# Mamba mixers: the skip term moved from VectorE to TensorE and ScalarE, lent scans in place

## What is computed

```
xc, z = split(h @ inproj);  xc = silu(causal_conv(xc) + convb)
dt = softplus(x_proj part @ dtw + dtb);  Bm, Cm = other parts of x_proj
per time step:  dA = exp(dt * A);  h = dA * h + (dt * xc) * Bm;  y = sum over n of h * Cm
y = y + xc * D
y = y * silu(z);  out = y @ outproj
```

## Time and profile before

| | |
|---|---|
| median of 3 runs | 2694.64 us |
| profiled execution | 2695.85 us, span 2694.0 us |
| first Mamba stage, scans | from 66 us to 991 us of the span |
| second Mamba stage, scans | from 1974 us to 2434 us |
| a chunk, first scan to first scan of the next | 115.0 us (odd chunks, scans begin at a state) to 119.7 us (even) |
| busy shares of the span | TensorE 88%, VectorE 69%, ScalarE 50%, GpSimd 57% |

### The profile page before, as it was taken

How to read it: one execution, slowest core, us unless ns; L and a number is a source line. 1 busy time by engine, 2 the same in 40 slices (tenths; PEclk the granted TensorE clock), 3 DMA queues, 4 the chain that set the end, 5 groups by cost and what they waited for, 6 DMA issues and landing times. The chain is left out here.

```text
span 2694.0 us, 28358 instructions
## 1 busy us (share of the span) xinstructions
PE 2361.3 (88%) x8874; PEld 1077.4 (40%) x8874; DVE 1870.9 (69%) x2587; ACT 1339.3 (50%) x2213; POOL 1543.2 (57%) x1356
## 2 busy tenths in 40 slices
PE   7989899898988778888999769999889989688878
PEld 3323333333333223343433349998433333223322
DVE  2999999999999983347777241111379999994334
ACT  4556565655656443444666423332266556453333
POOL 2999999999999971150000112222179999992010
PEclk9999999999999999999999979999789999999989
DMA  4030412303031100043121059996332130300000
GB/s 179 25 125 1 143 52 84 133 10 125 1 125 52 74 0 24 19 123 63 38 39 25 6 188 329 327 329 233 105 126 79 48 125 1 125 1 22 1 9 32
DMA packets 70204, 239.03 MB, mean 89 GB/s; under 512 B 15819, under 2 KB 35799, under 8 KB 47399
## 3 DMA queue, kind: packets, MB, share of 16 engines
q1 hardware_dynamic: 58292, 183.90, 20.3%
q10 hardware_dynamic: 8018, 43.09, 4.6%
q0 software_dynamic: 3744, 10.23, 1.0%
HBM read 220.60 MB, written 16.38 MB: 88 GB/s over the span
## 5 line engine op out<-in xcount | busy, mean ns | idle before, releaser
L896 POOL TENSOR_TENSOR s_dbu<-s_dx,s_bc 128x512 f32<-128x512 f32 x768 | 968.6, 1290 | 26.4 <-DVE s_psum L564 24.8
L480 PE MATMUL s_psum<-s_hc,ident 128*128 128x512 f32 x1536 | 831.1, 634 | 151.9 <-DVE s_hc L584 131.2
L759 ACT ACTIVATE s_psum<-s_dt,s_a_neg 128x512 f32<-128x512 f32 x768 | 521.7, 688 | 576.9 <-DVE s_hc L584 576.0
L480 PEld LDWEIGHTS s_psum<-s_hc,ident 128*128 128x128 f32 x1536 | 263.8, 193 | 657.7 <-DVE s_hc L584 413.8
L584 DVE TENSOR_TENSOR s_hc<-s_psum,s_bc 128x512 f32<-128x512 f32 x624 | 419.8, 673 | 0.4 <-issue 0.4
L564 DVE TENSOR_TENSOR_SCAN s_psum<-s_psum,s_state,s_dbu 128x512 f32<-128x512 f32 x312 | 394.6, 1277 | 11.4 <-POOL s_dbu L896 6.7
L564 DVE TENSOR_TENSOR_SCAN s_psum<-s_psum,s_dbu 128x512 f32<-128x512 f32 x312 | 381.4, 1223 | 14.9 <-POOL s_dbu L896 12.5
L2015 ACT ACTIVATE s_probs<-s_banks 128x512 f32<-128x512 f32 (+3 forms) x384 | 169.6, 495 | 117.1 <-PE s_banks L1724 85.8
L2452 ACT ACTIVATE s_hidden<-s_banks,s_w 128x128 f32<-128x128 f32 x312 | 97.6, 364 | 194.3 <-PE s_banks L2244 192.5
L163 POOL TENSOR_TENSOR s_pair<-s_res 128x512 f32<-128x512 f32 x4 | 5.1, 1280 | 328.5 <-issue 327.1
L907 POOL TENSOR_TENSOR s_hc<-s_hs,s_bc 128x512 f32<-128x512 f32 x144 | 183.6, 1275 | 14.6 <-DVE s_hs L564 14.6
(11 more groups left out here) (325 smaller groups left out, 3272.6 us busy)
## 6 DMA issues: line engine op xcount, KB each, us to landing
s_bc<-fwd_rows SPq DMA_DIRECT2D x64, 1024.0 KB, 4.7
s_w<-in_moe_w SPq DMA_DIRECT2D x39, 1028.0 KB, 5.9
s_w<-in_moe_w ACTq DMA_DIRECT2D x39, 1024.0 KB, 6.8
s_bc<-m_rows SPq DMA_DIRECT2D x32, 1024.0 KB, 4.7
qk_parts<-s_parts SPq DMA_DIRECT2D x48, 128.0 KB, 1.9
s_stack_q<-qk_parts SPq DMA_DIRECT2D x96, 64.0 KB, 2.4
s_stack_k<-qk_parts SPq DMA_DIRECT2D x48, 128.0 KB, 4.4
x<-in_xT SPq DMA_DIRECT2D x4, 512.0 KB, 6.7
```

Of the source, the lines that this page charges most:

```text
L480: pe.matmul(psum[:, SCANS + block_no % 2, :], consts["ident"][:], hc[:, unit % PRODUCTS, :], start=(n == 0), stop=(n == NS - 1)).then_inc( ...
L759: act.activation(psum[:, unit % SCANS, :], dt[:, g % 2, i // NS, :], ACT.Exp, scale=a_neg[CHUNKS[g][0]][:, i:i + 1]).then_inc(decay_ready, 1)
L896: pool.tensor_tensor(dbu[:, unit % TERMS, :], dx[:, g % 2, i // NS, :], bc[:, 2 * n, :], ALU.mult)\
```

## The change

TensorE adds the skip: after the 16th product of a block it multiplies u with a 128x128 diagonal matrix of D, from a new tile `skip_in` with the four diagonals of a run, into the same PSUM sum. ScalarE's new `store_sum` copies the sum to dx, at i = 7, 23, 39 and 55 and once at the end; VectorE's `skip` is gone. `skip_in` is loaded by SP at the stage's start and, in the first stage, again for the second run. The lent scans write over their term in `dbu` and `hs` is gone; VectorE no longer waits before them. The term that takes a lent unit's slot, the next instruction of GpSimd after its lent product, waits for that product. The fourth gate product moves from i = 9 to i = 11.

```diff
+            sp.dma_start(skip_in[:], dram[f"{first}_skip"]).then_inc(skip_loaded, 16)
             sp.dma_start(w_out[:], dram[f"{first}_out"]).then_inc(out_loaded, 16)
...
             for g in range(NC):
+                if g and g % PER_RUN == 0:
+                    sp.wait_ge(skip_used, EB * g)
+                    sp.dma_start(skip_in[:], dram[f"{runs[CHUNKS[g][0]][0]}_skip"]).then_inc(skip_loaded, 16)
...
                 pe.matmul(psum[:, SCANS + block_no % 2, :], consts["ident"][:], hc[:, unit % PRODUCTS, :],
-                          start=(n == 0), stop=(n == NS - 1)).then_inc(product_used, 1)
+                          start=(n == 0), stop=False).then_inc(product_used, 1)
+                if n == NS - 1:
+                    e = block_no % EB
+                    pe.wait_ge(skip_loaded, 16 * (CHUNKS[g][0] + 1))
+                    pe.matmul(psum[:, SCANS + block_no % 2, :], skip_in[:, e, :], u[:, g % 2, e, :], start=False, stop=True)\
+                      .then_inc(skip_used, 1)
...
-                if LENT[i] and lent(unit):
-                    dve.wait_ge(product_lent, lent(unit))
-                dve.tensor_tensor_scan(hs[:] if LENT[i] else h, h, dbu[:, unit % TERMS, :], begin, ALU.mult, ALU.add)\
+                dve.tensor_tensor_scan(dbu[:, unit % TERMS, :] if LENT[i] else h, h, dbu[:, unit % TERMS, :], begin, ALU.mult, ALU.add)\
...
-            def skip(block_no):
-
-                g, e = block_no // EB, block_no % EB
-                dve.wait_ge(product_used, NS * (block_no + 1))
-                dve.scalar_tensor_tensor(out=dx[:, g % 2, e, :], in0=u[:, g % 2, e, :],
-                                         scalar=cols[CHUNKS[g][0]][:, 2, e:e + 1], in1=psum[:, SCANS + block_no % 2, :],
-                                         op0=ALU.mult, op1=ALU.add).then_inc(y_read, 1)
...
-                    if i % NS == 3 and unit >= NS:
-                        skip(unit // NS - 1)
...
+            def store_sum(block_no):
+                act.wait_ge(skip_used, block_no + 1)
+                act.activation(dx[:, block_no // EB % 2, block_no % EB, :], psum[:, SCANS + block_no % 2, :], ACT.Copy)\
+                   .then_inc(y_read, 1)
...
                     decay(g, i)
+                    if i % NS == 7 and g * UNITS + i >= NS:
+                        store_sum((g * UNITS + i) // NS - 1)
...
                 if unit >= TERMS:
                     pool.wait_ge(scanned, unit - TERMS + 1)
+                    if LENT[(unit - TERMS) % UNITS]:
+                        pool.wait_ge(product_lent, lent(unit - TERMS + 1))
...
-                    pool.tensor_copy(state[:, i:i + 1], hs[:, CH - 1:CH]).then_inc(kept_lent, 1)
-                pool.tensor_tensor(hc[:, unit % PRODUCTS, :], hs[:], bc[:, 2 * (i % NS) + 1, :], ALU.mult)\
+                    pool.tensor_copy(state[:, i:i + 1], dbu[:, unit % TERMS, CH - 1:CH]).then_inc(kept_lent, 1)
+                pool.tensor_tensor(hc[:, unit % PRODUCTS, :], dbu[:, unit % TERMS, :], bc[:, 2 * (i % NS) + 1, :], ALU.mult)\
...
-                    if g and i in (3, 5, 7, 9):
-                        times_gate(g - 1, (i - 3) // 2)
+                    if g and i in (3, 5, 7, 11):
+                        times_gate(g - 1, (3, 5, 7, 11).index(i))
...
+    skips = np.zeros((P, EB, P), np.float32)
+    skips[np.arange(P), :, np.arange(P)] = skip.reshape(EB, P).T
```

More of the change, by code:

```diff
@@ L268, in mixers @@
         xd = s.sb("xd", [XD, CH])
-        hs = s.sb("hs", [P, CH])
+        skip_in = s.sb("skip_in", [P, EB, P])
         state = s.sb("state", [P, UNITS])
@@ L294, in mixers @@
         product_lent, kept_lent = s.sem("product_lent"), s.sem("kept_lent")
+        skip_loaded, skip_used = s.sem("skip_loaded"), s.sem("skip_used")
         squared, rstd_ready, normed, x_added = (s.sem("squared"), s.sem("rstd_ready"), s.sem("normed"),
@@ L638, in _ @@
             weigh(NC * UNITS - 1)
-            skip(NC * EB - 1)
             if post is not None:
@@ L825, in _ @@
                         store_x(g + 2, (i - 57) // 2)
+            store_sum(NC * EB - 1)
             for m in range(KD):
@@ L2711, in mamba_arrays @@
     x[BC0:XD] = xproj[rank:].reshape(2, NS, EI).transpose(1, 0, 2).reshape(2 * NS, EI)
+    skips = np.zeros((P, EB, P), np.float32)
+    skips[np.arange(P), :, np.arange(P)] = skip.reshape(EB, P).T
     return {
-        f"{name}_in": rows(inproj.T), f"{name}_x": rows(x.T), f"{name}_dt": dtw.T,
+        f"{name}_skip": skips, f"{name}_in": rows(inproj.T), f"{name}_x": rows(x.T), f"{name}_dt": dtw.T,
         f"{name}_out": rows(outproj.T),
```

## The result

The changed kernel takes 2702.51 us (median of 20 runs, 2696.39 to 2709.58) against 2695.56 of the kernel before (20 runs, 2692.36 to 2701.36): ratio 1.0026, 95% interval 1.0019 to 1.0033. It is slower by some 7 us. The prediction said 2690.7, with a range up to 2701.

The account below looks back on a forecast made before the run. It took each chunk's path to alternate between VectorE (units 10 to 42) and GpSimd, with VectorE and ScalarE at even chunks' ends. Terms per chunk summed to -3.9 us: 2690.7 from the median 2694.64, range 2681 to 2701.

Parts of the forecast that it names:

- The gates that it named: Waits at units 9, 10, 23, 45 and 56, and GpSimd from 42 into the next chunk, limit VectorE's gain.
- Its terms for units 19, 35 and 51: Removed sums: 19 gives 0.1 to 0.2, 35 up to 0.64, 51 0 or 0.14; last chunks 1.28 at 19 and 35.
- "-0.64" for unit 35: Odd chunks: removing the sum at 35 gains a full 0.64 us for the path leaving VectorE at 42.
- off the path after 42: From unit 42 GpSimd carries the path over the chunk's end to about 10 or 13 of the next.
- the 0.64 of which it had kept half: Unit 45: TensorE's added matmul delays ScalarE's decay chain, eating the 0.64 us; 0.3 to 0.4 taken for this branch.
- The self-wait: GpSimd's term waits for its own lent product: 0.12 us each, bounds 0 and 0.30; 0.60 a chunk at 45, 49, 5, 9, 13.
- The ends: End of each Mamba stage: matmul 0.86 and copy 0.57 replace VectorE's sum, +0.75 us, twice.
- TensorE's matmuls "at nothing": 48 added matmuls of 0.86 us cost nothing outside unit 45, as VectorE does not wait for TensorE.
- VectorE or GpSimd waiting for TensorE's sums: One of the listed signs, to be seen in the profile after, that the forecast is wrong.
- The other zero terms: Gate product moved from 9 to 11, lent scans over their terms, three 256 KB loads of diagonals: 0 each.
- The slower rival: Self-wait takes the place of the sums: at 0.30 us the sum is +5.1, 2699.7; chance 0.16.
- Its addition: TensorE's second added matmul pushes the logarithm at 44 past GpSimd's relu sums at 47: 0.3 us in 6 chunks, 2702.

Follow-up runs that it names:

- The skip alone: Kernel before with the skip as TensorE matmul (identity, D taken as 1) and ScalarE copy in place of VectorE's sum, lent scans as before: 2693.53 us, ratio 0.9987.
- the sums cut: Kernel before with VectorE's four skip sums of a chunk cut to one column each, nothing added elsewhere: 2683.67 us, ratio 0.9956.
- the gate product at 11: Kernel before with nothing but the fourth gate product moved from unit 9 to 11: 2696.01 us, ratio 1.0002.
- the matmuls of 16 and of 512 columns: Kernel before with one more TensorE matmul per block of sums, overwritten by the next: 2699.81 us with 16 columns, 2698.85 us with 512.

## Why the prediction was wrong

The gates that it named stood where it put them, one that it had excluded came into being (TensorE), and it summed -3.9 us where +7 came. By its own steps:

- **What the sums of VectorE are worth.** Its terms for units 19, 35 and 51 add up to 10.3 us in the scans, with ScalarE's and TensorE's share already taken off. The skip alone gave 7.6. The last chunks are right (1.48 each forecast, 1.46 and 1.44 found), the odd ones of the first stage are not: 0.74 each forecast, 0.58 found with the sums cut, and with the skip alone they are 0.2 longer than before. So "-0.64" for unit 35 failed there, twice over. GpSimd, which takes over at 42, waits for TensorE at that very unit (0.69 us with the skip alone), and VectorE, which the prediction took as off the path after 42, then waits for ScalarE 0.82 us at 45 and 1.17 at 56 and never again for a term. The odd chunk of the second stage has no variance matmuls on TensorE, no wait for TensorE at 42 and none for ScalarE at 45; there the skip alone gave 0.65 of the 0.74. The waits for ScalarE are where it looked for them; in the timeline of the changed kernel, chunk 1, VectorE waits at 23 for as much as forecast, and at 45 for all of the 0.64 of which it had kept half:

```profile
224.59 2.47 DVE L572 TENSOR_TENSOR_SCAN s_psum<-s_psum,s_state,s_dbu 128x512 f32<-128x512 f32 x2 [0.67 <-ACT s_psum L761]
...
260.81 1.29 DVE L572 TENSOR_TENSOR_SCAN s_psum<-s_psum,s_state,s_dbu 128x512 f32<-128x512 f32 x1 [0.67 <-ACT s_psum L761]
```

- **The self-wait** was the term "I take 0.12". It counted 4.9 us for it (41 waits); the changed kernel lies 6.5 us above the skip alone in the scans, which is 36 waits of 0.18. The price was a third too low. The count comes out near, though the sum leaves out the last chunk of each stage, where the waits cost 0.6 us each (110.9 us in the changed kernel, 110.3 with the skip alone); its rivals reckon with 50. The rows offered 0.12 and 0.30; the row chosen has a subtraction in bf16 and a memset, not two products in f32. With both terms the scans come to -1.1 in place of -5.4: odd chunks are 115.4 instead of 115.0, where 114.9 was forecast.
- **The ends**, +0.75 each. At the second one the copy ends 4.12 us after the last scan's end (2442.91 and 2438.79), VectorE's sum did so 3.42 after the earlier trace rows: +0.70, as predicted. On top, the granted clock was at half under the output projection:

```profile
2444.34 1.27 PE L501 MATMUL s_psum<-s_res,ident 128*128 128x512 f32 x2 [2.07 <-issue]
2445.41 5.16 PE L502 MATMUL s_psum<-s_dx,s_w_out 128*128 128x512 f32 x8
```

  The same eight records took 3.60 us before, so +1.56. The windows show it by the granted clock (the number before the last two): 0.76 in this one of the changed kernel, 1.00 in the one of before.

```profile
2442.50:2447.50 5.00, 3.16 (x5) 1.50 (x6) 0.00 (x0) 0.41 (x1) 1.26 (x1) 0.76 0.00 0
```
```profile
2437.80:2442.80 5.00, 3.88 (x9) 1.82 (x10) 0.00 (x0) 0.00 (x0) 1.02 (x1) 1.00 0.00 0
```

  Both profiles of the changed kernel have it here, neither of before; but so have three kernels in which VectorE still makes the sum (the gate product at 11, the matmuls of 16 and of 512 columns: 5.28 or 5.29 us, second end 20.3). So it is no effect of the copy in the chain. TensorE had stood idle about as long ahead of it in both (2.07 and 2.23 us), and why it falls here is not settled.
- **TensorE's matmuls "at nothing"** is the step that cost most. As work they make GpSimd wait 0.34 us at unit 42 in three chunks, 1.0 us in all (it is part of the scans above); "VectorE or GpSimd waiting for TensorE's sums" was among the prediction's own signs of being wrong. On top of the kernel before, the same matmuls cost nothing as work (16 and 512 columns come out alike), since VectorE was later there. As code they cost 2 to 4 us by the medians: +3.2 and +2.2 when their number is added to the kernel before, -3.1, -2.5 and -4.4 when it is filled up to a whole packet. Each of the last three is a difference of two medians that is uncertain by 2 to 4 us; what carries them is that all point the same way and that the rows are late in every profile with half a packet more and in none of the others. No part of the prediction looked at the instruction queues.
- The other zero terms hold: the gate product at 11 (+0.04), the loads of the diagonals (2702.96 without them).

The sum of what was found is 4.3 in the scans, some 1.6 at an end (seen in the profiles), 2 to 4 by code: 8 to 10 of the 11.8 us between forecast and median. Of what is left, 0.9 is the median of before itself, which three runs gave as 2694.64 and twenty as 2695.56. The slower rival named the right mechanism and the right terms, but at 0.30 us; at the 0.18 found, its own sum is -0.9, and it would not have come out slower either. Its addition, TensorE's second added matmul, was near as well, but what came late was the lent product of 42 and not the relu sums at 47, which wait for nothing. Its times, 2699.7 and 2702, lie close to the measured 2702.5 by luck.

## What to carry to other kernels

Work taken off an engine is worth what the gates behind it let through (10 of 24 us here), so price it by cutting the operation down before building its replacement. An engine for which nobody waits may be a few tenths from the path: what is added to it has to be checked in the kernel in which the other engines are already faster, since on top of the old one it seems free. An in-place operation saves a buffer, but puts a wait on the engine's own last instruction; put other work between the two. When a stage that wasn't touched changes its time, look at the instruction queues' packets beside the short DMAs that an engine waits for, and shift the program by part of a packet before blaming the change.

## What the hardware showed

- GpSimd waiting for its own previous instruction: 1.41 us from start to start where 1.23 is usual, for a product of 128x512 in f32; hidden by one other instruction between them.
- A 4 KB DMA that lands after 1.7 to 1.8 us took 3.1 to 3.7 when a 16 KB packet of TensorE's program was moved in the same microseconds.
- 192 TensorE instructions with next to no work in them changed a 2.7 ms kernel by +3.2 us, and by -4.4 in another one, in which they even cost 2 us in the scans (1383.4 against 1381.5).
- The granted clock of TensorE falls to half at places that differ from execution to execution of one kernel, worth 1.6 to 1.7 us each when a projection of eight records lies under it (5.36 against 3.70).
